# Graph attention with residual and layer norm: a second buffer for the result rows, and ScalarE's copies spread between the comparisons of one step

## The reference

```python
xt  = einsum('ni,hio->hno', x, W)                  # x 8192x256, W 4x256x64
src = einsum('hnf,hf->hn', xt, a[:, :64])
dst = einsum('hnf,hf->hn', xt, a[:, 64:])
e   = leaky_relu(src[:, :, None] + dst[:, None, :], 0.2)
e   = where(adj > 0, e, -inf)                      # adj 8192x8192 int32
att = softmax(e, axis=2)
h   = einsum('hij,hjf->hif', att, xt)              # heads side by side: 8192x256
out = layernorm(x + h)                             # eps 1e-5
```

## Time and profile before

| what | value |
|---|---|
| three runs | 2365.97, 2369.20, 2369.42 us, median 2369.2 |
| the profiled execution | 2367.08 us, of which the span of instructions is 2364.6 |
| busy in the span | PE 2108.9 (89%), DVE 2098.4 (89%), ACT 2012.6 (85%), POOL 120.0 (5%) |
| mean granted clock of TensorE | 0.962 of 2.4 GHz |
| the chain that ended last | PE 48%, ACT 16%, DVE 14%, issue 8%, POOL 2% |
| DMA | 469.77 MB, 199 GB/s mean |

### The profile page before, as it was taken

The page is one execution under the profiler, slowest core; times in us unless marked ns, Lnnn a source line. Parts: engine busy times, 40 slices in busy tenths (PEclk is TensorE's granted clock), DMA queues, the critical chain, the costliest instruction groups (busy, mean ns, idle before and its releaser), DMA issues.

```text
span 2364.6 us, 79642 instructions
## 1 busy us (share of the span) xinstructions
PE 2108.9 (89%) x34180; PEld 2063.9 (87%) x34180; DVE 2098.4 (89%) x2334; ACT 2012.6 (85%) x2045; POOL 120.0 (5%) x88
## 2 busy tenths in 40 slices
PE   7602999998999899998999999998999899998996
PEld 6502999998999899998999999998999899998996
DVE  4597999998999899998999899998999899987785
ACT  2235798898999899998999899998999899999995
POOL 0062000001000100001000100001000100001000
PEclk9855999999999999999999999999999999999998
DMA  8647776766666576666666576666666576533210
GB/s 296 221 180 284 275 247 231 241 218 213 209 200 221 176 239 208 209 202 212 211 199 209 188 236 205 213 203 209 210 203 221 176 236 206 194 84 105 84 52 19
DMA packets 236588, 469.77 MB, mean 199 GB/s; under 512 B 14656, under 2 KB 23104, under 8 KB 236224
## 3 DMA queue, kind: packets, MB, share of 16 engines
q1 hardware_dynamic: 231600, 447.53, 57.3%
q0 software_dynamic: 4352, 16.78, 2.0%
q10 hardware_dynamic: 272, 0.13, 0.0%
HBM read 438.83 MB, written 25.56 MB: 196 GB/s over the span
## 4 chain that ended last, share of the span: by engine, by line
PE 48%; ACT 16%; DVE 14%; issue 8%; POOL 2%; DVEq 0%; POOLq 0%; ACTq 0%
PE acc L754 46%; ACT big L392 15%; DVE big L560 4%; DVE big L567 4%; PE tp L719 2%; DVE nat L482 1%; ACT big L411 1%; DVE stats L613 1%; POOL shift L330 1%; DVE big L552 1%; DVE big L582 1%; DVE nat L480 1%; POOL rstd L329 0%; DVE AT L496 0%; DVE big L589 0%
## 5 line engine op out<-in xcount | busy, mean ns | idle before, releaser
L754 PE MATMUL acc<-big 128*128 128x130 f16 x32768 | 1933.5, 221 | 84.1 <-DVE big L567 53.7
L754 PEld LDWEIGHTS acc<-big 128*128 128x128 fp8e5 x32768 | 1901.0, 98 | 107.2 <-issue 103.6
L392 ACT ACTIVATE big<-big,d_all 128x1024 int8<-128x1024 f32 x1792 | 1881.4, 1139 | 60.9 <-PE acc L754 58.4
L560 DVE SCALAR_TENSOR_TENSOR big<-big,AT 128x1024 uint32<-128x1024 uint32 x512 | 627.4, 1225 | 168.6 <-ACT big L392 157.7
L567 DVE SCALAR_TENSOR_TENSOR big<-AT,big 128x1024 uint32<-128x1024 uint32 x512 | 627.0, 1225 | 4.5
L719 PE MATMUL tp<-ident,nat 128*128 128x128 f32 x1024 | 158.8, 278 | 133.0 <-DVE nat L480 115.9
L719 PEld LDWEIGHTS tp<-ident,nat 128*128 128x128 f32 x1024 | 109.7, 142 | 142.9 <-issue 132.5
L552 DVE TENSOR_SCALAR big<-big,d_all 128x1024 uint8<-128x1024 f32 x256 | 193.2, 755 | 0.0
L480 DVE TENSOR_SCALAR nat<-raw 128x2048 fp8e4<-128x2048 int32 x128 | 177.0, 1386 | 6.9 <-DMA raw<-in_adj_dram 6.5
L482 DVE TENSOR_SCALAR nat<-raw 128x2048 uint8<-128x2048 int32 x128 | 177.8, 1389 | 0.0
L496 DVE SCALAR_TENSOR_TENSOR AT<-AT,tp 128x512 uint32<-128x512 uint32 x224 | 154.8, 691 | 1.5
(11 more groups left out here) (48 smaller groups left out, 364.2 us busy)
## 6 DMA issues: line engine op xcount, KB each, us to landing
raw<-in_adj_dram SPq DMA_DIRECT2D x256, 1024.0 KB, 5.4
big<-v_parts SPq DMA_DIRECT2D x512, 260.0 KB, 3.8
v_parts<-big SPq DMA_DIRECT2D x16, 1040.0 KB, 4.2
big<-s_rows SPq DMA_DIRECT2D x32, 512.0 KB, 5.8
AT<-in_x_dram SPq DMA_DIRECT2D x16, 512.0 KB, 4.0
big<-in_x_dram POOLq DMA_DIRECT2D x8, 1024.0 KB, 7.6
out_dram<-big POOLq DMA_DIRECT2D x8, 1024.0 KB, 7.9
big<-in_L_gnn_W_dram SPq DMA_DIRECT2D x2, 128.0 KB, 2.6
```

The costliest lines, as they stand in the source:

```text
L392: ins = nc.scalar.activation(sgn[:, g % NB, b, :], srow[:, h % 2, :], ACT.Sign, bias=dflat[:, r:r + 1], scale=-1.0)
L560: nc.vector.scalar_tensor_tensor(out=word(sgn, g % NB), in0=word(sgn, g % NB), scalar=EDGE[plane], in1=edges(g), op0=ALU.bitwise_and, op1= ...
L754: return nc.tensor.matmul(acc[:, k, o:o + 2 * VO], m[:, g % NB, b, t * P:(t + 1) * P], Vr[:, v:v + 2 * VO], start=opens, stop=False, skip_ ...
```

## The change

`y` becomes two buffers of 2048 words, chosen by the chunk's parity, with a semaphore each for the load of x. POOL loads x for chunks 0 and 1 at the start. After the store of chunk c it loads x for chunk c + 2 into the same buffer. ACT's `normalise` of the chunk before moves from steps 12 to 15 of the first pass (two tiles each) to steps 8 to 15 of the second pass (one tile each). The three parts of `low` of the pass before move from behind the comparisons of step 1 to between those of step 2: part b follows comparison b, for b = 0, 1, 2, and comparison 3 follows part 2. DVE's order, PE and SP are unchanged. The loops of ACT and POOL run over two chunks per turn.

```diff
-        big = sb("big", [P, 24144], fp32)
+        big = sb("big", [P, 26192], fp32)
...
-        y = words(12416, 2048).rearrange("p (t f) -> p t f", t=T)
+        y = [words(start, 2048).rearrange("p (t f) -> p t f", t=T) for start in (12416, 24144)]
...
-            load_res(0)
-
-            def chunk(c):
-                deviation(c - 1)
-                store(c - 1)
-                pool.wait_ge(out_done, 16 * c)
-                load_res(c)
-
-            with pool.Fori(1, NC) as c:
-                chunk(c)
-            deviation(NC - 1)
-            store(NC - 1)
+            load_res(0, 0)
+            load_res(1, 1)
+
+            def chunk(c, n):
+                deviation(c)
+                store(c, n)
+
+                pool.wait_ge(out_done, 16 * c + 16)
+                load_res(c + 2, n)
+
+            with pool.Fori(0, NC // 2 - 1) as i:
+                chunk(2 * i, 0)
+                chunk(2 * i + 1, 1)
+            for c in (NC - 2, NC - 1):
+                deviation(c)
+                store(c, c % 2)
...
-            def signs(n, g, h):
-                act.wait_ge(sums_done, n + 1)
-                for b in range(scalar_blocks(g)):
-                    r = (g * B + b) * H + h
-                    ins = nc.scalar.activation(sgn[:, g % NB, b, :], srow[:, h % 2, :], ACT.Sign,
-                                               bias=dflat[:, r:r + 1], scale=-1.0)
-                ins.then_inc(sgn_done, 1)
+            def sign(g, h, b):
+                r = (g * B + b) * H + h
+                return nc.scalar.activation(sgn[:, g % NB, b, :], srow[:, h % 2, :], ACT.Sign,
+                                            bias=dflat[:, r:r + 1], scale=-1.0)
...
-            def chunk(c, first=False):
+            def chunk(c, n, first=False):
                 for h in range(H):
                     p = c * H + h
                     act.wait_ge(row_in[h % 2], 32 * c + 16 * (h // 2 + 1))
                     for g in range(NG):
-                        signs(p * NG + g, g, h)
-                        if g == 1 and not (first and h == 0):
-                            for part in range(3):
-                                low(p - 1, part)
-                        if g in (12, 13, 14, 15) and h == 0 and not first:
-                            normalise(c - 1, (2 * g - 24, 2 * g - 23))
+                        act.wait_ge(sums_done, p * NG + g + 1)
+                        for b in range(scalar_blocks(g)):
+                            ins = sign(g, h, b)
+                            if b == scalar_blocks(g) - 1:
+                                ins.then_inc(sgn_done, 1)
+                            if g == 2 and b < 3 and not (first and h == 0):
+                                low(p - 1, b)
+                        if h == 1 and g >= 8 and not first:
+                            normalise(c - 1, 1 - n, (g - 8,))
...
-            def add_on(p, ec, eh):
+            def add_on(p, ec, eh, n):
 
-                dve.wait_ge(res_in, 16 * ec + 16)
+                dve.wait_ge(res_in[n], 8 * (ec - n) + 16)
```

More of the change, by code:

```diff
@@ L145, in gat_residual_norm @@
         added = sem("added")
[L146 removed]
+        res_in = [sem("res_in0"), sem("res_in1")]
         stats_done = sem("stats_done")
@@ L333, in deviation, with store @@
                 nc.gpsimd.tensor_tensor(out=shift[:, :], in0=shift[:, :], in1=rstd[:, :], op=ALU.mult).then_inc(shift_done, 1)
[L335 removed]
+            def store(c, n):
                 pool.wait_ge(norm_done, T * c + T)
[L337 removed]
+                pool.dma_start(out_v[c], y[n]).then_inc(out_done, 16)
             pool.wait_ge(lo_done, NG + 2)
             pool.wait_ge(U2_done, 2 * NG)
[L341 to L352 removed]
+            load_res(0, 0)
[11 more added lines that the diff above has]
+                store(c, c % 2)
             pool.wait_ge(out_done, 16 * NC)
@@ L406, in low, with normalise @@
                 ins.then_inc(low_done, 1)
-            def normalise(c, ts):
+            def normalise(c, n, ts):
                 act.wait_ge(shift_done, 2 * c + 2)
                 for t in ts:
-                    nc.scalar.activation(y[:, t, :], y[:, t, :], ACT.Identity, bias=shift[:, t:t + 1],
+                    nc.scalar.activation(y[n][:, t, :], y[n][:, t, :], ACT.Identity, bias=shift[:, t:t + 1],
                                          scale=rstd[:, t:t + 1]).then_inc(norm_done, 1)
-            def chunk(c, first=False):
+            def chunk(c, n, first=False):
                 for h in range(H):
@@ L428, in _ @@
             act.wait_ge(U2_done, 2 * NG)
-            chunk(0, first=True)
-            with act.Fori(1, NC) as c:
-                chunk(c)
+            chunk(0, 0, first=True)
+            with act.Fori(0, NC // 2 - 1) as i:
+                chunk(2 * i + 1, 1)
+                chunk(2 * i + 2, 0)
+            chunk(NC - 1, 1)
             for part in range(3):
                 low(NP - 1, part)
-            normalise(NC - 1, range(T))
+            normalise(NC - 1, (NC - 1) % 2, range(T))
         @block.vector
@@ L600, in divide, with moments @@
                                         in1=rden[:, :].unsqueeze(2).broadcast_to([P, T, O]), op=ALU.mult).then_inc(tr_done, 1)
-            def add_on(p, ec, eh):
-                dve.wait_ge(res_in, 16 * ec + 16)
+            def add_on(p, ec, eh, n):
+                dve.wait_ge(res_in[n], 8 * (ec - n) + 16)
                 dve.wait_ge(tr_done, p + 1)
                 u4 = u.rearrange("p (t c) v -> p t c v", c=2)
-                yh = y[:, :, eh * O:(eh + 1) * O]
+                yh = y[n][:, :, eh * O:(eh + 1) * O]
                 nc.vector.tensor_tensor(out=yh, in0=yh, in1=u4[:, :, 1, 0:O], op=ALU.add).then_inc(added, 1)
-            def moments(c, ts):
+            def moments(c, n, ts):
                 dve.wait_ge(added, 4 * c + 5)
                 for t in ts:
-                    nc.vector.bn_stats(stats[:, t, :], y[:, t, :]).then_inc(stats_done, 1)
+                    nc.vector.bn_stats(stats[:, t, :], y[n][:, t, :]).then_inc(stats_done, 1)
             def spread(c):
@@ L664, in chunk @@
                             if g == 6:
-                                add_on(p, ec, eh)
+                                add_on(p, ec, eh, 1 - plane if h == 0 else plane)
                         if h == 0 and not first:
                             if g == 8:
-                                moments(c - 1, range(0, 4))
+                                moments(c - 1, 1 - plane, range(0, 4))
                             if g == 9:
-                                moments(c - 1, range(4, T))
+                                moments(c - 1, 1 - plane, range(4, T))
                             if g == 10:
@@ L686, in _ @@
             divide(NP - 1)
-            add_on(NP - 1, NC - 1, H - 1)
-            moments(NC - 1, range(T))
+            add_on(NP - 1, NC - 1, H - 1, 1)
+            moments(NC - 1, 1, range(T))
             spread(NC - 1)
```

4 lines of the change are left out of this document (2 added, 2 removed).

## The result

The changed kernel takes 2277.9 us (median of 4 runs, 2274.59 to 2280.18) against 2368.7 before (4 runs): ratio 0.9618, 95% interval 0.9601 to 0.9634, so 90.8 us faster where 99 were forecast. The profiled execution took 2278.14 us with a span of 2275.9, 88.7 less than the span before.

A forecast was written before the change was run, and what follows sets the result against it. PE (247.5 us) and DVE (247.7) nearly bound the 266.0 us chunk, the rest being loss. A chunk of 251.0 saves 90 us over six, passes 1 to 3 save 3, the last chunk 6: 99 in all, 2270 us (2250 to 2306).

The forecast's parts named there:

- The boundary: At pass boundaries, moved copies let DVE start step 2 2.6 us earlier; 2.3 us of loss goes into passes 3 and 0.
- The count of copy after comparison: ACT's step 2 timed from comparison 0's start with copies between: comparison 3 ends at 5.8 us, before at 8.3.
- The first pass: First pass, 13.0 us over 61.9: moving normalisation removes ACT's 9.06 us wait for `shift`, PE's 3.44 us stop and the slow clock.
- The load at the start: Prologue: the second load of x brings data wanted a chunk later; no change forecast before pass 1.
- The moments: First pass: DVE's moments and spread, 3.2 us, cost 1.5 us (0 to 3.2) near step 10 and 0.25 at its end.
- it lands 1.5 us after PE wants it: First pass: step 10's second mask from DVE lands at 44.2 us where PE wants it at 42.7.
- ACT behind after the second pass: Boundary after the normalising second pass: ACT comes 2.6 us late to step 2, costing 1.8 us (0 to 3.5).
- 0.8 not yet made up: Second pass: some 0.8 us ACT still lags since the boundary, added to 2.2 us by step 15: 3.0 behind the ring.
- The last chunk: Last chunk, without conversions, 247.3 us before: 241 forecast, saving 6 us (3 to 9).
- PE at its own pace: Rival: the ring covers everything, a chunk is 247.5 us, total 2245 us; chance 0.12 (chunk under 249).
- DVE as the bound: Rival: nothing covers DVE's work, a chunk is 255 us, total 2297 us; chance 0.26 (chunk 253.5 to 259).
- The two slower ones: Rivals: late copies stop PE at each pass start, 2413 us, chance 0.02; Sign/Copy turns reload tables, 2509 us, chance 0.01.

The follow-up runs named there:

- copies_only: Kernel before with only the copies of low sums moved between step 2's comparisons; normalisation and single result buffer as before: 2324.1 us, ratio 0.9822.
- normalise_only: Changed kernel with the low copies back behind step 1's comparisons, keeping two buffers and the moved normalisation: 2320.3 us, 0.9805 of the kernel before.
- late_load: Changed kernel with POOL's load of x for chunk 1 issued only after three passes (48 steps), not at the start: 2272.5 us.
- all_three: Changed kernel with late_load, dve_unrolled and moments_spread, plus normalising in every fourth step of second and third passes: 2263.4 us.
- moments_left_out: all_three with DVE's moments taken from 8 of 256 columns, so part of the computation is left out: 2247.1 us, chunk 248.2 us.
- dve_unrolled: Changed kernel with DVE's hardware loop over chunks 2 to 5 written out, so no jump back at chunk 4: 2274.3 us.
- copies_late: Changed kernel with all three low copies behind step 2's comparisons instead of between them: 2338.6 us, 0.9883 of the kernel before.
- moments_three_passes: all_three with moments over three passes, spread in the third pass's step 13, normalisation in the fourth and next first pass: 2249.3 us.
- three_and_early: moments_three_passes with DVE's additions of high sums placed around step 1's first mask at the start of fourth passes: 2246.9 us.
- moments_spread: Changed kernel with DVE's moments two at a time in steps 7, 9, 11, 13 of the first pass, spread in step 15: 2274.8 us.

## Why the prediction was right, and where it was off

- *The boundary.* DVE 2.6 us earlier at step 2, passes with ACT ahead at 61.9 (DVE's wait fell by 2.3 us, from 2.87 to 0.54): shown by the timeline and by copies_only, whose chunk came out within 0.2 us of the count. The count of copy after comparison was right to 0.15 us.
- *The first pass.* The wait for `shift`, PE's stop and the slow clock went together: 13.0 us of loss became 1.5. normalise_only shows this part alone.
- *The load at the start.* "The second load at the start brings data that are wanted a chunk later" was true and beside the point. The step that failed is that I asked when its data are needed and not what its transfer stands in front of. Cost 2.6 us in the first pass, shown by late_load and by the first passes of all the traces.
- *The moments.* 1.5 + 0.25 us were forecast as a peak at step 10. The size was off, and so was the place: all_three, in which ACT comes in time, still has 250.3 - 247.5 = 2.8 us a chunk over PE's pace, and 2.1 of them go with 2.0 us of the moments' work (moments_left_out). The step "it lands 1.5 us after PE wants it" looked at the masks alone and not at `high`, for which PE has no ring of four slots. The upper bound, all 3.2 us of it, was near the truth.
- *ACT behind after the second pass.* 1.8 us forecast, 1.4 to 1.6 measured. The "0.8 not yet made up" was wrong: ACT waited 0.33 us for PE in front of step 8, so it had caught up.
- *DVE's jump back.* Not in the sum. The trace before had it, with its name, 3.69 us long; I didn't look for a stop that was hidden by a wait which the change removes, here DVE's at step 2. 2.4 to 2.6 us, shown by dve_unrolled.
- *The last chunk.* 4.2 us instead of 6. The trace has a stop of PE of 2.84 us there, described below; late_load, without one, has 239.6 us for this chunk where 241 was forecast.
- *The near hit.* 251.7 for 251.0 is in part luck: ACT's share was taken 0.4 us too high and the moments' about 1 us too low, and these partly cancel.
- *Slips.* DVE was free at 701.25 + 0.96 = 702.2 and not 702.1, a chunk of 249 gives 2258 and not 2256, and 2270 + 495 is 2765. None of them moves the forecast.
- *The rivals.* PE at its own pace was 4.3 us a chunk away, DVE as the bound 3.3. The two slower ones did not occur; copies_late shows that the first of them was a question of two or three comparisons. Of the table loads the groups by line say after the change what the earlier trace rows said before it:

```profile
L367 ACT ACT_TABLE_LOAD x8 | 10.3, 1283 | 42.0 <-PE acc L708 42.0
```

Eight, all in the prologue, and none at the 186 turns between Sign and Copy. The Trainium skill, "ScalarE: Activation LUTs", section "Table sets: the hidden batching unit", says in the second half of its rule that copy is in every set, and the trace agrees. The 2.66 us stand in the Trainium skill, "ScalarE: Activation LUTs", section "What ACT_TABLE_LOAD costs"; no run here shows a switch among the chunks.

## What to carry to other kernels

Give each hand-over at a stage's end its place by both sides' clocks: the same four copies cost 42 us more behind the comparisons of step 1, and 61 us more behind those of step 2, than between them. One can count one such delay from a timeline to a few tenths of a microsecond; two delays at one boundary are not to be added (normalise_only). Before a wait is removed, look for stops that it hides today (a jump, a peak of another engine), and for every new transfer ask what is queued at that moment as well as when its data are used. Where engines are within 1% of each other, as here, work was free only pass by pass: split it until no stretch holds more than its room, instead of moving the peak.

## What the runs showed of the hardware

PE stops where its loop for the last chunk begins, after 34 matmuls of the first pass, and the profile names nothing that it waits for. In the changed kernel's trace this is 2.84 us:

```profile
2015.88 60.09 PE L760 MATMUL acc<-big 128*128 128x130 f16 x1024 [2.84 <-issue]
```

It was 2.87 in all_three and 3.40 in moments_three_passes, 0.38 to 0.71 in eight others (0.67 before), and none shows in late_load, three_and_early and copies_late, though PE's program is the same in all. The pass takes 62.9 us in the changed kernel and 63.2 in all_three, but 59.4, 59.2 and 58.9 in moments_spread, dve_unrolled and late_load, with nearly the same work. That is near the 5 us by which runs of one kernel spread. There is one trace of each kernel, so whether the stop goes with the kernel or with the execution, and whether the runs without a profile differ for this reason, is not shown.

VectorE stands 3.0 to 3.7 us at the jump back of its loop (dve_unrolled), and in the changed kernel's trace the view names ACT for it.
